# Two-layer decoder on one core: work moved between stages, softmax sums inverted by way of DRAM

## What is computed

```
layer 0: x += rwkv(layernorm(x))                    # time mixing
         x += banded attention over features        # xattn0, uses ctx as encodings
         x += ternary MLP (weights quantised per 64 elements)
layer 1: x += causal attention, 16 heads            # attn1
         x += attention, q from x, k and v from ctx # xattn1
         x += 2 of 8 experts (each 256 wide)
```

```
scores = einsum('bqhd,bkhd->bhqk', q, k) / sqrt(d)
attn   = softmax(where(band, scores, neg))    # band in xattn0 alone
o      = einsum('bhqk,bkhd->bqhd', attn, v)
```

```
scale = clip(mean(|w_g|), 1e-08);  q = clip(round(w_g / scale), -1, 1)
w_hat = w + (q * scale - w)        # in bf16
```

## Time and profile before

| what | value |
| --- | --- |
| median of three timed runs | 2652.47 us (2649.92 to 2655.51) |
| the profiled execution | 2666.59 us, its span 2664.7 us |
| busy in the span: TensorE (PE), its weight loads (PEld) | 2238.8 us (84%), 1625.4 us (61%) |
| DVE, ACT, POOL | 1828.5 (69%), 1153.3 (43%), 898.1 (34%) |
| mean DMA rate over the span | 69 GB/s |

### The profile page before, as it was taken

How to read it: one execution, slowest core, us unless ns; L and a number is a source line. 1 busy time by engine, 2 the same in 40 slices (tenths; PEclk the granted TensorE clock), 3 DMA queues, 4 the chain that set the end, 5 groups by cost and what they waited for, 6 DMA issues and landing times. The chain is left out here.

```text
span 2664.7 us, 54852 instructions
## 1 busy us (share of the span) xinstructions
PE 2238.8 (84%) x19596; PEld 1625.4 (61%) x19596; DVE 1828.5 (69%) x4630; ACT 1153.3 (43%) x2616; POOL 898.1 (34%) x1507
## 2 busy tenths in 40 slices
PE   3777849999999992899988999599999997188695
PEld 3666626777777761899977777354555554155463
DVE  4999976777777768455555666678888886144255
ACT  1222215555555552222226666366666664032231
POOL 2555542222222213566650100233323330415322
PEclk8888869999999995899999999799999998599898
DMA  4000023443333320000000210235443340113434
GB/s 115 1 0 1 1 50 93 116 115 86 100 86 100 86 64 0 2 2 2 2 2 1 105 53 1 51 107 166 141 115 112 110 111 26 66 56 106 147 94 160
DMA packets 245916, 183.14 MB, mean 69 GB/s; under 512 B 28800, under 2 KB 237872, under 8 KB 244880
## 3 DMA queue, kind: packets, MB, share of 16 engines
q1 hardware_dynamic: 230640, 136.77, 19.1%
q0 software_dynamic: 10848, 38.67, 4.2%
q10 hardware_dynamic: 4160, 4.19, 0.5%
HBM read 94.47 MB, written 83.51 MB: 67 GB/s over the span
## 5 line engine op out<-in xcount | busy, mean ns | idle before, releaser
L773 ACT ACTIVATE xattn_pr<-ps 128x384 f32<-128x384 f32 (+1 forms) x1024 | 536.2, 541 | 380.7 <-PE ps L503 224.0
L644 DVE TENSOR_REDUCE xattn_mx<-ps 128x2 f32<-128x512 f32 (+1 forms) x768 | 465.7, 633 | 173.3 <-PE ps L488 90.8
L485 PE MATMUL ps<-xattn_kp,xattn_qp 96*128 96x192 bf16 (+1 forms) x2048 | 395.5, 265 | 47.9 <-DMA xattn_kp<-xattn_rows 27.0
L500 PE MATMUL ps<-xattn_qp,xattn_kp 128*128 128x192 bf16 (+1 forms) x2048 | 409.7, 262 | 11.8 <-ACT xattn_pr L773 7.1
L518 PE MATMUL ps<-xattn_pr,xattn_vs 128*32 128x256 f32 (+1 forms) x4096 | 306.7, 371 | 0.5 <-ACT xattn_o L778 0.3
L500 PEld LDWEIGHTS ps<-xattn_qp,xattn_kp 128*128 128x128 bf16 x2048 | 179.3, 97 | 156.4 <-ACT xattn_pr L773 79.8
L485 PEld LDWEIGHTS ps<-xattn_kp,xattn_qp 96*128 96x128 bf16 x2048 | 191.7, 99 | 91.0 <-issue 29.8
L503 PE MATMUL ps<-xattn_band,xattn_ident 128*128 128x192 bf16 x1024 | 210.4, 246 | 0.0
L1013 PE MATMUL ps<-ffn_parts,gate_up_t 128*128 128x128 bf16 x3072 | 194.2, 220 | 2.1 <-DVE ffn_parts L1131 2.1
L1013 PEld LDWEIGHTS ps<-ffn_parts,gate_up_t 128*128 128x128 bf16 x3072 | 184.1, 99 | 16.4 <-DVE ffn_parts L1131 2.5
L848 POOL TENSOR_TENSOR xattn_rest<-xattn_qk,xattn_parts 128x512 f32<-128x512 f32 x64 | 74.0, 1156 | 351.8 <-ACT xattn_parts L796 351.8
(11 more groups left out here) (313 smaller groups left out, 4644.2 us busy)
## 6 DMA issues: line engine op xcount, KB each, us to landing
xattn_rows<-xattn_parts SPq DMA_DIRECT2D x128, 192.0 KB, 2.1
xattn_qp<-xattn_rows SPq DMA_DIRECT2D x256, 96.0 KB, 2.8
xattn_kp<-xattn_rows SPq DMA_DIRECT2D x256, 96.0 KB, 3.1
xattn_rows<-xattn_parts SPq DMA_DIRECT2D x128, 128.0 KB, 2.1
moe_rows_in<-region_zero POOLq DMA_DIRECT2D x6, 1677.0 KB, 8.0
moe_xb<-moe_rows_in SPq DMA_DIRECT2D x78, 129.0 KB
xattn_rows<-xattn_parts SPq DMA_DIRECT2D x128, 64.0 KB, 1.8
moe_row<-moe_rows_out SPq DMA_DIRECT2D x16, 512.0 KB, 8.5
```

Of the source, the lines that this page charges most:

```text
L485: mm = nc.tensor.matmul(out, qp[u][s][0:R_MAX, h, mt * P:(mt + 1) * P], kp[u][s][0:R_MAX, h, lo:lo + width], start=True, stop=not by_product)
L500: mm = nc.tensor.matmul(out, kp[u][s][:, h, nt * P:(nt + 1) * P], qp[u][s][:, h, lo:lo + width], start=True, stop=not banded)
L644: ins = nc.vector.tensor_reduce(mx[s][:, h * NT:(h + 1) * NT], of, AX.X, ALU.max)
L773: nc.scalar.activation(out, src, ACT.Exp, scale=HD ** -0.5).then_inc(exped, 1)
```

## The change

- The ternary arithmetic moves into xattn0. A class `Ternary` works on one set per three pairs, from pair 9 on: ACT casts at head 1, DVE does one of nine steps at heads 2, 6 and 12; the two steps that POOL did are DVE's now. The old stage keeps the transposes, eight in a PSUM bank, and one wide copy per set, by DVE and ACT in turn.
- The softmax sums, one row per head, no longer go through an alignment product and a reciprocal over 128 partitions and 256 columns. `o_sb` is stored to DRAM, the sums alone are loaded as 128 x 32, inverted (`invert`, head 8), stored, and loaded again with each row spread over eight partitions into `rden`; `normal_o` (head 13) waits for that. The four DMAs are in SyncE's queue; the second half of `place` comes behind them. Two alignment products remain, both at head 4. To have the sums in rows of their own, heads are laid out in the order `TURN`, the values are copied in four pieces, and `C_SELECT` is half as large.
- In xattn0 TensorE adds the band for 4 of 16 heads, before for 8; the gate product moves to head 15, the output product, the gate and the new x to the step after (heads 3, 1 and 5), and the context is loaded a pair later.
- In xattn1 the new x moves to head 15, `round_1` and `round_2` from heads 7 and 9 to 9 and 12.
- The experts' weights are loaded in attn1 from pair 18 on, no longer in xattn1.

```diff
+    TERNARY_FROM = 9
+    TERNARY_AT = 2, 6, 12
...
-            return h % 2 == 1
+            return h % 4 == 3
...
+                def store_outputs(p):
+                    sp.wait_ge(o_kept, p + 1)
+                    wait(sp, sums_in, 16 * p)
+                    sp.dma_start(o_rows, o_sb[:].rearrange("p a b -> p (a b)")).then_inc(o_stored, 16)
+
+                def load_sums(p):
+                    sp.wait_ge(o_stored, 16 * (p + 1))
+                    wait(sp, inverted, p)
+                    src = o_rows.rearrange("(g r) x -> g r x", g=QUAD)[:, SUM_ROW:SUM_ROW + 2, :].rearrange("g r (k i) -> g r k i", i=NHS * D // P)
+                    sp.dma_start(sums[:], src).then_inc(sums_in, 16)
+
+                def store_inverses(p):
+                    sp.wait_ge(inverted, p + 1)
+                    wait(sp, inv_in, 16 * p)
+                    sp.dma_start(inv_rows.rearrange("h (k i) -> (h k) i", i=NHS * D // P), inv[:]).then_inc(inv_stored, 16)
+
+                def load_inverses(p):
+                    sp.wait_ge(inv_stored, 16 * (p + 1))
+                    wait(sp, normal, p)
+                    src = inv_rows.rearrange("h (a x) -> h a x", a=1).broadcast_to([NHS, HD, D])
+                    sp.dma_start(rden[:], src).then_inc(inv_in, 16)
...
+                    if not first:
+                        store_outputs(p - 1)
                     if there(p + 2):
                         place(p + 2, u, 0)
+                    if not first:
+                        load_sums(p - 1)
                     if not last:
                         place_maxima(p + 1, 1 - u, 0)
+                    if not first:
+                        store_inverses(p - 1)
+                        load_inverses(p - 1)
                     if there(p + 2):
                         place(p + 2, u, 1)
-                    if banded and not last:
-                        load_context(p + 1, 1 - u)
+                    if banded and not first:
+                        load_context(p, u)
...
+                def align(p):
+                    pe.wait_ge(o_kept, p + 1)
+                    wait(pe, normal, p)
+                    for half in range(2):
+                        at = C_SELECT + half * P
+                        mm = nc.tensor.matmul(ps[:, BANK_N, 0:D], c[:, at:at + P], o_sb[:, half, :],
+                                              start=(half == 0), stop=(half == 1))
+                    mm.then_inc(aligned, 1)
...
-                        if j in ALIGNED and not first:
-                            for half in range(2):
-                                align(p - 1, 2 * ALIGNED.index(j) + half)
+                        if j == ALIGNED and not first:
+                            align(p - 1)
...
-                        if banded and not first and j == 11:
+                        if banded and not first and j == 15:
                             gate_product(p - 1)
-                        if banded and not first and j == 13:
-                            out_product(p - 1)
+                        if banded and p >= 2 and j == 3:
+                            out_product(p - 2)
...
-                def reciprocal_sums(p, half):
-
-                    v.wait_ge(aligned, nth(p, 2, 2))
-                    wait(v, normal, nth(p - 1, 3, 3))
-                    x = slice(half * P, (half + 1) * P)
-                    nc.vector.reciprocal(rden[:, x], ps[:, BANK_N, D + half * P:D + (half + 1) * P]).then_inc(normal, 1)
+                def invert(p):
+
+                    v.wait_ge(sums_in, 16 * (p + 1))
+                    wait(v, inv_stored, 16 * p)
+                    nc.vector.reciprocal(inv[:], sums[:]).then_inc(inverted, 1)
 
                 def normal_o(p):
 
-                    v.wait_ge(normal, nth(p, 3, 2))
+                    v.wait_ge(aligned, p + 1)
+                    v.wait_ge(inv_in, 16 * (p + 1))
...
+                        if j in TERNARY_AT and ternary_set(p) is not None:
+                            ternary.step(nc, v, ternary_set(p), 3 * ((p - TERNARY_FROM) % 3) + TERNARY_AT.index(j))
                         if j == 4 and not last:
                             values(p + 1, 1 - u)
                         if j == (5 if banded else 3) and there(p + 3):
                             normalise_q(p + 3, 1 - u)
-                        if j in (7, 8) and not first:
-                            reciprocal_sums(p - 1, j - 7)
-                        if j == 9 and not first:
+                        if j == 8 and not first:
+                            invert(p - 1)
+                        if j == 13 and not first:
                             normal_o(p - 1)
-                        if j == 11 and not first and not banded:
+                        if j == 15 and not first and not banded:
                             new_x(p - 1, 1 - u)
-                        if j == 11 and not first and banded:
-                            gate_by_context(p - 1, 1 - u)
-                        if j == 14 and not first and banded:
-                            new_x(p - 1, 1 - u)
+                        if j == 1 and p >= 2 and banded:
+                            gate_by_context(p - 2, u)
+                        if j == 5 and p >= 2 and banded:
+                            new_x(p - 2, u)
...
+                        if j == 1 and ternary_set(p) is not None and (p - TERNARY_FROM) % 3 == 0:
+                            ternary.cast(nc, a, ternary_set(p))
                         if j == 8 and not last:
                             keep_maxima(p + 1, 1 - u, 0)
                         if there(p + 3):
                             if banded and j == 10:
                                 projections(p + 3, 1 - u)
-                            if j == (11 if banded else 7):
+                            if j == (11 if banded else 9):
                                 round_1(p + 3, 1 - u)
-                            if j == (13 if banded else 9):
+                            if j == (13 if banded else 12):
...
+    def cast(self, nc, act, i):
+        act.wait_ge(*self.landed)
+        wait(act, self.made, nth(i, self.STEPS, 0))
+        nc.scalar.activation(self.half[:], self.nat[:, i, :], ACT.Copy).then_inc(self.halved, 1)
+
+    def step(self, nc, v, i, k):
+        groups = lambda t: t.rearrange("p (g w) -> p g w", w=GROUP)
+        spread = lambda t: t.rearrange("p (g a) -> p g a", a=1).broadcast_to([P, WIDE // GROUP, GROUP])
+        half, a, b, total, scale, thr, nthr = (t[:] for t in (self.half, self.a, self.b, self.total, self.scale, self.thr, self.nthr))
+        if k == 0:
+            v.wait_ge(self.halved, i + 1)
+        wait(v, self.made, nth(i, self.STEPS, k))
+        if k == 0:
+            ins = nc.vector.tensor_reduce(total, groups(half), AX.X, ALU.add, apply_absolute_value=True)
+        elif k == 1:
+            ins = nc.vector.tensor_scalar(scale, total, 1.0 / GROUP, self.FLOOR, ALU.mult, ALU.max)
+        elif k == 2:
+            nc.vector.tensor_scalar(thr, scale, 257.0 / 512, None, ALU.mult)
+            ins = nc.vector.tensor_scalar(nthr, scale, -257.0 / 512, None, ALU.mult)
+        elif k == 3:
+            ins = nc.vector.tensor_tensor(groups(a), groups(half), spread(thr), ALU.is_gt)
+        elif k == 4:
+            ins = nc.vector.tensor_tensor(groups(b), groups(half), spread(nthr), ALU.is_lt)
+        elif k == 5:
+            ins = nc.vector.tensor_tensor(a, a, b, ALU.subtract)
+        elif k == 6:
+            ins = nc.vector.tensor_tensor(groups(b), groups(a), spread(scale), ALU.mult)
+        elif k == 7:
+            ins = nc.vector.tensor_tensor(a, b, half, ALU.subtract)
+        else:
+            ins = nc.vector.tensor_tensor(self.quant[:, i, :], half, a, ALU.add)
+        ins.then_inc(self.made, 1)
...
+                for i in range(0, TERNARY_SETS, 2):
+                    v.wait_ge(turned, i + 1)
+                    nc.vector.tensor_copy(*evict(i))
...
+                for i in range(TERNARY_SETS):
+                    for k in range(per):
+                        mm = nc.tensor.transpose(ps[:, i, k * P // 2:(k + 1) * P // 2].bitcast(BF16), quant[:, i, k * P:(k + 1) * P], ident[:])
+                    mm.then_inc(turned, 1)
...
+                    if 0 <= p - LATER_FROM < len(later[0]):
+                        to, of = later[0][p - LATER_FROM]
+                        g.dma_start(to, of).then_inc(later[1], 16)
...
+            ternary = Ternary(core, own, rows, (landed, 16 * len(loads)))
+            wide_attention(core, "xattn0", i['ctx_2048'], wide, later=(loads, landed), ternary=ternary)
...
-            wide_attention(core, "xattn1", i['ctx_2048'], later=(loads, landed))
+            with ExitStack() as stage:
+                regions = Regions(core, stage)
+                causal_attention(core, "attn1", attn, b_q, b_k, b_v, b_o, regions, later=(loads, landed))
+            core.end_stage()
+
+
+            wide_attention(core, "xattn1", i['ctx_2048'])
```

184 lines of the change are left out of this document (80 added, 104 removed).

## The result

The changed kernel takes 2608.32 us (median; 2603.06 to 2612.56, four runs) where the kernel before takes 2652.32 (2649.92 to 2655.51). The ratio is 0.9832, 95% interval 0.9812 to 0.9853: 44 us faster. I had forecast 67 and 2585.5; the range, 2530 to 2635, holds the result, the forecast's own narrower one, 2565 to 2605, misses it by 3.

The account below looks back on a forecast made before the run. Both cross attentions run at TensorE's pace, and the ternary stage is DVE and POOL arithmetic. Terms -50 - 47 + 21 + 6 + 10 - 7 = -67 took the median 2652.5 to 2585.5 us; range 2530 to 2635.

Parts of the forecast that it names:

- xattn0, TensorE: In xattn0, fewer alignment products and band matmuls save 1.5 us per pair, 19.0 to 17.5, times 31: -47 us.
- xattn0, ternary arithmetic: Ternary steps on DVE in xattn0 stall TensorE 1.0 us in 18 pairs, plus 3 for casts: +21 us.
- sums by way of DRAM, xattn1: In xattn1, four transfers in SyncE's queue make DVE, then TensorE, wait: 0.2 us more per pair, +6 over 31.
- tails: After each cross attention's last pair nothing covers the chain, 9.3 us for 4.5: +4.8 twice, +10 us.
- It holds if nothing else is late: Condition on xattn0's 17.5 us pair; DVE, losing two reciprocals and gaining a smaller one, was held not to be late.
- 0 taken, bounds 0 and +1 per pair: In xattn0 the inverses land at +16.3 of 17.5 us, TensorE needs them some 1.2 later: no cost.
- xattn1's T: Period of a pair in xattn1: 15.8 us, from 14.45 + 0.8 + (16.3 - T); landings give 15.1 to 16.2.
- The formula's floor: In xattn1, late left-overs on POOL ending at 13.3 and a 1.15 us split keep the next transpose from before 14.45.
- the second rival: Ternary steps and POOL's splits hold each other up, nearly all 45 us exposed: 24 more, 2610 us; chance 0.23.
- The first rival: The chain arrives in time: T in xattn1 is 14.2, 1.6 less than forecast, -50: 2535 us; chance 0.22.
- the third (2772): Rival: DRAM round trips each about 1.2 us later than taken, in both cross attentions, +186: 2772 us; chance 0.06.
- The estimate of 8.9: By the skill's DMA figures the chain's four transfers take 8.9 us, against the prediction's 8.2 without queueing.

Follow-up runs that it names:

- the two later profiles: The kernel before and the changed kernel, both unchanged, each profiled a second time: spans of 2652.3 and 2607.5 us.
- the late version with SyncE's issues: The fast version with the store and load of the inverses back in SyncE's queue, all heads kept: 2564.68 us.
- the first late version: Changed kernel with the inversion moved from head 8 to 11 and the multiplication by the inverses to the next step: 2587.15 us.
- the run with the sums first: Changed kernel with SyncE issuing the output's store and the load of the sums ahead of the placing: 2597.29 us.
- the fast version: The first late version with the inverses' store and load issued from ACT's queue, and inversion, gate and new x one to two heads later: 2537.14 us.
- ACT at head 9: Changed kernel with its own heads, the inverses' store and load issued from ACT's queue at heads 9 and 12: 2698.76 us.

## Why the prediction was right or wrong

| term | forecast | measured | by |
|---|---|---|---|
| ternary stage | -50 | -51 | stage, 6.9 for 57.8 |
| xattn0, TensorE | -47 | -47 | 17.49 for 19.00 x 31, where DVE takes the sums late |
| xattn0, ternary arithmetic | +21 | +12 to +14 | 18.64 and 18.75 for 17.96, x 18 |
| xattn0, pairs 2 to 8 | 0 | +8 to +11 | 19.12 and 19.51 for 17.96, x 7 |
| xattn0, every pair | 0 | +15 | 17.96 for 17.49, x 31 |
| sums by way of DRAM, xattn1 | +6 | +16 | 556.2 for 535.9, less 4 of tail |
| tails | +10 | +10 | 11.6 to 17.0, 9.4 to 13.6 |
| experts' loads | -7 | -11 | 535.9 for 546.8 |
| sum | -67 | -48 to -43 | the two later profiles: -45 |

The rows are differences of single profiles, and some compare kernels that differ in more than the term: 17.49 is of the late version with SyncE's issues, which also has other heads.

**Right to a few us**: the ternary stage, TensorE's share of xattn0, both tails, and the direction of the loads, which hold up a pair or two at either side more than I counted. attn1 took them for nothing.

**The step that failed first** is "It holds if nothing else is late", with "so it isn't" for DVE. I added up DVE's operations, which got fewer, and did not ask which of them now stand beside each other. Even in pairs without ternary steps and without loads the period is 17.96, not 17.5. There TensorE stops once a pair, 0.46 us, for the maxima behind the block of q's normalisation and the new x, both at head 5, and 0.36 for the split of the maxima; it stops for 0.19 in the late version with SyncE's issues. The stop of 0.46 is the same with the sums' load ahead of the placing, where DVE does not wait for the sums (17.97 a pair). In the first late version, without either wait of DVE's, the period is 17.85. So of the 0.47 above 17.49 the chain can have little, some 0.1 by these; the rest I put down to DVE's order, which no run changes alone.

**The chain in xattn0** is the second: "0 taken, bounds 0 and +1 per pair", and "no slower pairs 2 to 8". I compared only the last landing with the end of the pair, and not the first one with DVE's place in its program: DVE asks for the sums at head 8, and waits there, over 430 to 580 us, while POOL issues the ternary loads, and over 905 to 970 in the changed kernel:

```profile
DVE xattn_inv L703 <- DMA xattn_sums<-xattn_o_rows: 17.1, 8, 3.2
...
DVE xattn_inv L703 <- DMA xattn_sums<-xattn_o_rows: 2.4, 3, 1.1
```

That is 2.1 us in each of eight pairs, and 0.8 in each of three. In pairs 2 to 8 it costs 1.2 to 1.6 us each, above the upper bound: the first late version, with the same loads and no such wait, has 17.95 there. Some of it is TensorE's clock: in these seven pairs it stood at half for some 3 us in the first profile and 7 in the second, which costs at most half of that. In all others the wait costs little or nothing, as the run with the sums first shows.

**xattn1's T**, the period of a pair, was 16.46 (16.3 over the stage's middle) for 15.8, above my 16.2 for the latest landings. What the sum has at nothing is TensorE's clock: the prediction reads the granted clock of 0.97 and doesn't ask whether the stalls that it adds will lower it. The 27 us at half clock cost at most 14 in 27 pairs, 0.5 each, and the twenty without took 15.82. That agreement is part luck: the stretches follow long stalls, so the pairs without them are the ones that stalled least, and the version with the sums first has none in its middle and still takes 16.07, with other waits. Scatter is likely the other part, which is argued and not shown: I put landings in as one number each, and the inverses come at +15.1 to +18.1; a late pair stalls TensorE and an early one gives nothing back. The formula's floor was wrong too: I had 14.45 from the late rounding, and the fast version runs pairs at 14.05 with just that rounding, while undoing it changed nothing. TensorE's stalls behind DVE, 29.0 us in 19 pairs or 1.5 each, are near the 1.3 that the formula has (0.5 + 0.8).

**The ternary arithmetic** came out at 0.7 to 0.8 a pair for 1.0 taken, in the changed kernel. How much it costs hangs on its place among DVE's other work: 0.3 on the kernel before, 0.3 again in xattn0 of the late version with SyncE's issues (17.78 for 17.49). In the changed kernel TensorE waits behind the block of heads 5 and 6, where I had it, and also 0.45 us behind the ternary step at head 12 and line 713 at 13, where I hadn't. An example of the first, and the step of head 12 in the changed kernel and in the late version with SyncE's issues:

```profile
767.92 1.22 DVE L1373 TENSOR_TENSOR tern_b<-tern_half,tern_nthr 128x1024 bf16<-128x1024 bf16 x1
...
769.76 0.34 PE L533 MATMUL ps<-xattn_kp,xattn_qp 96*128 96x192 bf16 x2 [0.81 <-DVE xattn_mx L683]
...
L1375 DVE TENSOR_TENSOR tern_a<-tern_a,tern_b x6: 1200/1206/1208, 606.1 to 886.5; 128x1024 bf16<-128x1024 bf16 x6
...
L1374 DVE TENSOR_TENSOR tern_a<-tern_a,tern_b x6: 682/684/684, 595.3 to 862.4; 128x1024 bf16<-128x1024 bf16 x6
```

The same operation takes 1.21 in the one and 0.68 in the other. In the changed kernel POOL's subtraction (line 901, 1.16 us) has started 0.50 before it and the two overlap by 0.66. With two more lines stretched like this, the steps take DVE 53.8 us in all, for 44.6 in the late version. This is what the second rival names, at 9 us and not at 24. The row it went by shows less than the prediction took from it: line 1324, with its 2.09, reads one tensor, so it isn't a case of two inputs.

The second rival wants nearly all 45 us exposed, and 12 to 14 were: its number, 2610, is nearly the result, and its reason is not. That is worth a warning: the blind sum and a rival can both sit beside the measured time for the wrong cause. The first rival (the chain in time, 2535) came true as a kernel, at 2537, with its T of 14.2 nearly met (14.43), once DVE takes both landings late and SyncE need not wait for them. Against the third (2772): no landing was late by 1.2 in the mean.

The DMA landings in the changed kernel's xattn1, issue to landing: output, spread inverses, stored inverses (KB, median us).

```profile
xattn_o_rows<-xattn_o SPq DMA_DIRECT2D x24, 256.0 KB, 2.3
xattn_rden<-xattn_inv_rows SPq DMA_DIRECT2D x25, 128.0 KB, 2.5
...
xattn_inv_rows<-xattn_inv SPq DMA_DIRECT2D x25, 16.0 KB, 1.4
```

I had 2.2, 2.3 and 1.8. The Trainium skill (DMA: Bandwidth & Descriptors, "Anatomy of one DMA") names a fixed cost of about 2.0 us, by which the 16 KB store would take 2.0; here it took 1.4. The page states it for software descriptors, and for this store on SyncE's queue it is too high; but the same store took 2.1 in xattn1 with the sums first and 2.8 from ACT's queue in the fast version, so 1.4 isn't a constant either. The estimate of 8.9 worked out from it for the four compares with 1.4 + 2.5 + 2.3 and, for the load of the sums behind four placing transfers, 2.8 from issue to use: 9.0.

What was not tried: ACT's issues in xattn1 together with SyncE's in xattn0 (by stages, 8 us under 2537), the kernel before with old sums but fewer masks, and the new sums without the ternary steps, which would split xattn0's terms cleanly.

## What to carry to other kernels

Price a chain of transfers at each place where an in-order engine asks for it, not only at its end: what counts is whether the landing comes before that instruction's turn, and what stands queued behind it. Then look at what stands beside what in the busiest in-order engine: a sum of its busy time says nothing of two blocks in one head. Give waits for round trips distance in every queue that takes part, the issuing ones as well; a wait moved to another engine costs the same or more unless it finds its event already there (ACT at head 9: +90 us; at head 13 with a late DVE: -71). Ask too whether new stalls will lower TensorE's clock, and read it per pair, not per stage. And where a resource is freed but the period hardly moves, look for who is idle in front of whom: in xattn0, 45 us less TensorE work shortened the stage by 4 to 7.
